# First attention's softmax two tiles ahead with exponentials per head, and one bf16 product for an expert bias

## The reference

```python
x = x + tanh(g_xattn[0]) * xattn0(layernorm(x), ctx, ctx, mask, Wq, Wk, Wv, Wo, bo)
# xattn0: 16 heads of 64, 64 keys
dots = einsum('bhid,bhjd->bhij', qh, kh) * d ** -0.5
dots = where(mask, -finfo.max, dots)
attn = softmax(dots); out = einsum('bhij,bhjd->bhid', attn, vh) -> @ Wo + bo
```

```python
expert_out = dispatched @ w_expert + b_expert        # 256 x 256, bias of 256
combined = combine @ expert_out                       # gate * (location < 100)
```

## Time and profile before

| | us |
|---|---|
| median of 3 runs | 954.27 |
| lowest, highest | 948.47, 955.95 |
| profiled execution | 944.84 |
| its span | 943.1 |
| PE, DVE, ACT, POOL busy | 787.4, 630.2, 334.4, 283.0 |

### The profile page before, as it was taken

The page is one execution under the profiler, slowest core; times in us unless marked ns, Lnnn a source line. Parts: engine busy times, 40 slices in busy tenths (PEclk is TensorE's granted clock), DMA queues, the critical chain, the costliest instruction groups (busy, mean ns, idle before and its releaser), DMA issues.

```text
span 943.1 us, 13461 instructions
## 1 busy us (share of the span) xinstructions
PE 787.4 (83%) x4214; PEld 593.6 (63%) x4216; DVE 630.2 (67%) x1698; ACT 334.4 (35%) x622; POOL 283.0 (30%) x284
## 2 busy tenths in 40 slices
PE   7688988965788777589989799978999998779992
PEld 6455656653256656379978676635676675479971
DVE  3678889866997666555637775556757655566646
ACT  2422231225644662134544543312233221235530
POOL 1038113160001556614561111234001234205540
PEclk9998999997999999779999998889999998889995
DMA  8629950000001002247426000051000011224427
GB/s 284 123 92 385 313 187 0 1 1 1 0 1 34 1 0 86 95 122 248 137 80 223 1 1 1 1 179 34 1 1 12 35 45 47 89 58 143 134 85 255
DMA packets 55474, 83.30 MB, mean 88 GB/s; under 512 B 14688, under 2 KB 44384, under 8 KB 55136
## 3 DMA queue, kind: packets, MB, share of 16 engines
q1 hardware_dynamic: 48496, 63.52, 21.8%
q0 software_dynamic: 6912, 18.95, 5.6%
HBM read 61.41 MB, written 37.95 MB: 105 GB/s over the span
## 4 chain that ended last, share of the span: by engine, by line
PE 50%; DVE 24%; ACT 8%; DVEq 6%; issue 6%; DMA 3%; POOL 2%; SPq 0%; ACTq 0%; POOLq 0%
PE sh L701 12%; PE ob L701 12%; PE sh L1077 6%; PE ob L1077 6%; PE pt L669 4%; DVE sm L1801 2%; DVE x L2043 2%; DVE work L1805 2%; DVE work L1793 2%; DVE mx L1791 2%; ACT work L1340 2%; PE pt L701 2%; DVEq L1790 2%; DVE stats L1657 2%; PE pt L1069 2%
## 5 line engine op out<-in xcount | busy, mean ns | idle before, releaser
L701 PE MATMUL sh<-area,xnT 128*128 128x512 f32 (+1 forms) x384 | 138.2, 509 | 7.0 <-issue 4.5
L701 PE MATMUL ob<-area,work 128*128 128x256 f32 x512 | 116.3, 380 | 9.0 <-ACT work L1277 9.0
L534 POOL TENSOR_TENSOR rstd<-var,minush 128x4 f32<-128x4 f32 (+1 forms) x29 | 30.4, 1047 | 303.6 <-DVE var L1664 303.6
L701 PEld LDWEIGHTS ob<-area,work 128*128 128x128 f32 x512 | 96.7, 190 | 34.6 <-issue 22.8
L598 POOL DMA_INDIRECT yt<-xn,work x80 | 76.7, 959 | 122.5 <-ACT xn L1521 106.9
L701 PEld LDWEIGHTS sh<-area,xnT 128*128 128x128 f32 x384 | 64.3, 199 | 59.6 <-issue 56.4
L1340 ACT ACTIVATE work<-work 128x1024 f32<-128x1024 f32 x32 | 33.8, 1058 | 174.5 <-DVE work L1793 93.6
L589 POOL DMA_INDIRECT xg<-area,dest x64 | 63.9, 999 | 70.4 <-DVE dest L2035 53.0
L669 PE MATMUL pt<-ident,work 128*128 128x128 f32 (+1 forms) x292 | 41.9, 284 | 24.7 <-DVE work L1805 10.8
L701 PE MATMUL ob<-area 128*128 128x256 f32 (+1 forms) x152 | 45.2, 458 | 15.8 <-DVE area L2061 9.0
L669 PEld LDWEIGHTS pt<-ident,work 128*128 128x128 f32 (+1 forms) x292 | 33.8, 142 | 32.8 <-issue 14.4
(11 more groups left out here) (298 smaller groups left out, 1664.2 us busy)
## 6 DMA issues: line engine op xcount, KB each, us to landing
work<-xg SPq DMA_DIRECT2D x80, 129.0 KB, 2.3
area<-in_L_ffn_w SPq DMA_DIRECT2D x4, 2048.0 KB, 12.6
area<-yt SPq DMA_DIRECT2D x8, 1024.0 KB, 9.0
area<-in_L_xattn_Wq SPq DMA_DIRECT2D x2, 1024.0 KB, 9.7
x<-in_x SPq DMA_DIRECT2D x1, 2048.0 KB, 15.3
area<-in_L_xattn_Wo SPq DMA_DIRECT2D x2, 1024.0 KB, 16.0
area<-in_L_xattn_Wkv SPq DMA_DIRECT2D x2, 1024.0 KB, 6.3
out<-x SPq DMA_DIRECT2D x4, 512.0 KB, 2.9
```

Of the source, the lines that this page charges most:

```text
L534: pool.tensor_tensor(rstd[:, n], var[:, n], minush[:, n], ALU.pow).then_inc(given, 1)
L701: mm = pe.matmul(o, a, b, start=(k == 0), stop=(k == len(lhs) - 1))
```

## The change

It has two parts.

**First attention.** `attend16` and the exponential are split: stage 0 has functions of its own, stage 6 keeps the old work under the name `attend6`.

- `sh` fills 12 and 13 are now the scores of tiles 0 and 1, 14 to 21 the eight value fills, and from 22 (`FOLDED0`) on the numbers count as before. PE transposes block 0's tokens before the value folding and does the two tiles of scores there.
- DVE masks and takes maxima in two halves of 8 heads each, the first once PE's first half is there (`scored_half`). The maximum is written negated. The subtraction and the sum are gone.
- ACT does 16 exponentials of 128 x 64 a tile, each with the negated maximum as bias and the sum over keys as its accumulator output. The ones of tiles 0 and 1 run between its value evictions.
- In the loop DVE works on scores of tile i + 2 and normalises tile i + 1; both used to be tile i + 1. ACT's exponentials are of tile i + 2.
- `row_max` and `weight_scales` move from the value folding into tiles 0 to 3 of the loop; statistics of blocks 2 and 3 move forward by a few evictions; the next block's normalisation is done at the end of a block for the one after it.
- SP's wait is for `FOLDED0`, 22.

**Stage 5's bias.** In stage 3, after the tables and ahead of the first pair of expert tiles, DVE splits the bias into three bf16 parts, on partitions 0, 32 and 64 of a zeroed 96-row operand (`be2_parts`, in the memory of `bo0`). PE multiplies 96 rows of bf16 ones with it in one product in place of the float32 one of one row.

```diff
+        SCORES0, VALUES0, FOLDED0 = start_of("sh", 0) + 12, start_of("sh", 0) + 14, start_of("sh", 0) + 22
...
-            sp.wait_ge(sh_taken, start_of("sh", 0) + PRE["sh"][0])
+            sp.wait_ge(sh_taken, FOLDED0)
...
+            def scores16(stage, u, j):
+                n, slot = score_fill(stage, u, j)
+                sh_slot(n)
+                for c in range(2):
...
+                    if stage == 0 and c == 0:
+                        mm.then_inc(scored_half, 1)
+                mm.then_inc(sh_full, 1)
...
+                first_norm_T(6, 1)
+                pe.wait_ge(pt_moved, 8)
+                pe.wait_ge(sh_taken, SCORES0)
+                scores16(0, 0, 0)
+                scores16(0, 0, 1)
+                n = VALUES0
                 pe.wait_ge(in_o, loads)
...
             pe.wait_ge(pt_moved, start_of("pt", 5) + PRE["pt"][5])
+            pe.wait_ge(bias_split, 1)
...
-                                     [T(5, b)[:, k, j * P:(j + 1) * P] for k in range(KD)] + [ones[0:1, :]],
-                                     [wexp[:, k * D:(k + 1) * D] for k in range(KD)] + [be2[0:1, :]])
+                                     [T(5, b)[:, k, j * P:(j + 1) * P] for k in range(KD)] + [onesb[0:96, :]],
+                                     [wexp[:, k * D:(k + 1) * D] for k in range(KD)] + [be2_parts[0:96, :]])
...
+            def exps0(i, first, last):
+
+                act.wait_ge(shifted[0], 2 * i + (2 if last > H // 2 else 1))
+                for h in range(first, last):
+                    p = prob[i % 2][:, h * C:(h + 1) * C]
+                    a = act.activation(p, p, ACT.Exp, bias=mx[:, i % 2, h:h + 1], accum_out=sm[:, i % 2, h:h + 1])
+                if last == H:
+                    a.then_inc(exped[0], 1)
...
+                first_norm_move(6, 0)
+                exps0(0, 0, H // 2)
+                exps0(0, H // 2, H)
                 for m in range(MI):
-                    n = n0 + 12 + m
+                    n = VALUES0 + m
...
+                    if m < 4:
+                        exps0(1, 4 * m, 4 * m + 4)
+
+            def attend0():
+                for b in straight:
+                    for j in range(TB):
+                        i = b.u * TB + j
+                        for half in range(2):
+                            n = prob_fill(0, i, half)
+                            move(n, n % 2, probT[:, half * 512:(half + 1) * 512])
+                        if i + 2 < NT:
+                            exps0(i + 2, 0, H // 2)
+                        if j == 1 and b.u + 1 < NB:
+                            norm_move(0, b, 4)
+                        if i + 2 < NT:
+                            exps0(i + 2, H // 2, H)
...
+            def shift0(i):
+
+                n, slot = score_fill(0, i // TB, i % TB)
+                for c in range(2):
+                    q = slice(c * 512, (c + 1) * 512)
+                    p = prob[i % 2][:, q]
+                    dve.wait_ge(*((scored_half, i + 1) if c == 0 else (sh_full, n + 1)))
+                    ins = dve.scalar_tensor_tensor(heads(p), mask[:, i, :].unsqueeze(1).broadcast_to([P, H // 2, C]), -FMAX,
+                                                   heads(sh[slot][:, q]), ALU.mult, ALU.add)
+                    if c == 1:
+                        ins.then_inc(sh_taken, 1)
+                    dve.drain()
+                    dve.tensor_reduce(mx[:, i % 2, c * H // 2:(c + 1) * H // 2], heads(p), AX.X, ALU.max,
+                                      negate=True).then_inc(shifted[0], 1)
+
+            def normalise0(i):
+                p = prob[i % 2]
+                dve.wait_ge(exped[0], i + 1)
+                dve.reciprocal(rsm[:, i % 2, :], sm[:, i % 2, :])
+                dve.drain()
+                dve.tensor_tensor(heads(p), heads(p), over_keys(rsm[:, i % 2, :]), ALU.mult).then_inc(prob_ready[0], 1)
+
+            def attend0():
+                for b in straight:
+                    for j in range(TB):
+                        i = b.u * TB + j
+                        pb = Block(b.u - 1)
+                        if i >= 1:
+                            add(Block((i - 1) // TB), 0, (i - 1) % TB, [(i - 1) % TB])
+                        if i + 2 < NT:
+                            shift0(i + 2)
+                        if i + 1 < NT:
+                            normalise0(i + 1)
+                        if i < 3:
+                            row_max(i)
+                        if i == 3:
+                            weight_scales()
+                        if b.u >= 1 and j == 0:
+                            norm_stats(pb)
+                        if b.u >= 1 and j == 1:
+                            extremes(pb)
+                        if i == 0:
+                            norm_next(0, straight[0], xn_free(0, straight[0], 5))
+                        if j == 3 and b.u + 2 < NB:
+                            norm_next(0, straight[b.u + 1], xn_free(0, straight[b.u + 1], 5))
+                add(straight[-1], 0, TB - 1, [TB - 1])
+                norm_stats(straight[-1])
+                extremes(straight[-1])
...
+            def bias_parts():
+
+                dve.memset(be2_parts[:, :], 0.0)
+                for r, before in ((0, 0), (32, 1), (64, 2)):
+                    row, part = be2[r:r + 1, :], be2_parts[r:r + 1, :]
+                    for _ in range(before):
+                        dve.drain()
+                        dve.tensor_copy(part, row)
+                        dve.drain()
+                        dve.tensor_tensor(row, row, part, ALU.subtract)
+                    dve.drain()
+                    ins = dve.tensor_copy(part, row)
+                ins.then_inc(bias_split, 1)
...
             fold16(0, bo0, {5: lambda: first_stats(straight[0]), 8: lambda: first_stats(straight[1]), 9: first_norm,
-                            10: row_masks, 13: lambda: first_stats(straight[2]), 14: lambda: row_max(0),
-                            15: lambda: row_max(1), 16: lambda: row_max(2), 17: weight_scales,
-                            18: lambda: first_stats(straight[3])})
-            attend16(0)
+                            10: row_masks, 12: lambda: normalise0(0), 13: lambda: first_stats(straight[2]),
+                            15: lambda: first_stats(straight[3])})
+            attend0()
```

## The result

| | before | changed |
|---|---|---|
| median of the runs (us) | 953.74 (948.47 to 955.95, 4 runs) | 923.95 (915.80 to 925.28, 4 runs) |
| the profiled execution, its span (us) | 944.84, 943.1 | 925.28, 923.5 |

The ratio of the times is 0.968, 95% interval 0.961 to 0.975: the change takes 29.8 us away, and the time is 3 us under the forecast. A second series of the changed kernel has 921.79 us against 954.80, ratio 0.964 (0.959 to 0.970). The 954.80 is the median of eleven executions, three of which were slow (one took 4316.54 us); the other eight, which the ratio uses, have a median of 953.96. The two spans differ by only 19.6 us: the profiled execution of before was 9 us under the median of its kernel, and that of after was the longest of its four. So the traces are compared stretch by stretch.

The account below looks back on a forecast made before the run. VectorE was taken to bound the first attention's loop, TensorE stage 5. Savings 5.0 + 14.4 + 7.8 = 27.2 us took the span from 943.1 to 915.9; with 11.2 for the median, 927 us, range 916 to 942.

Parts of the forecast that it names:

- Part 1: First attention's loop: TensorE sets the pace at 7.76 us a tile, loop 125.0 us against 139.4, 14.4 us saved.
- The margin: Loop handoff: VectorE has the next tile's probabilities ready at 7.5 us, TensorE wants them at 7.76, a quarter microsecond spare.
- Rival (a): Loop: VectorE's handoff is late, 0.5 us a tile over, 7 us in all, giving 934 us; chance 0.16.
- rival (b): Loop: ScalarE becomes the bound, activation and accumulator read not overlapping, 0.52 us a pair, giving 949 us; chance 0.09.
- Part 2: Start, before the loop: first transposes at 69.3 us instead of 74.28, 5.0 us saved (2.3 to 7.3).
- the walk: Start: three engine queues followed through scores and value fills; fills end at 68.0, last eviction 69.2, first transposes 69.3.
- Rival (d): Start saving lost to value folding behind ScalarE's exponentials, or GpSimd 2 us late, giving 932 us; chance 0.07.
- Part 3: GpSimd's weight rounding: scales come about 102 instead of 59, last rounding 1.3 us late but covered, cost 0 (0 to 2).
- Part 4: Stage 5's bias product: one bf16 pass over 96 rows saves 0.48 us in each of 16 products, 7.8 us.
- the 0.17 us kept back for a change between kinds of product: Stage 5: deducted from the 0.65 us a product saving, for a cost of changing product kinds that stays.
- Rival (c): Stage 5: the bias product saves nothing, since switching between kinds of product may be what costs, giving 935 us; chance 0.08.
- The bias's split: Stage 3 on VectorE: some 4.5 us within an 8.72 us wait for gathered tokens; cost 0, or 4.5 without that wait.

Follow-up runs that it names:

- the experiment: One more half-width maximum, result unused, ahead of each reciprocal, against the changed kernel: loop 128.6 us instead of 124.8; whole kernel 924.53 us, a single execution, beside 957.31.
- the bias part alone: The kernel before with only stage 5's bias product changed (with its split into parts): 929.65 us beside 946.97, ratio 0.982.
- the repetition: The changed kernel, unaltered, run once more beside a further variant on the same chip: 921.79 us, ratio 0.964 to the kernel before.

## Why the prediction was right, and where its sum was not

**Part 1, the loop (14.4 us forecast, 14.6 measured).** The mechanism held: 7.76 us a tile, no wait at the handoff, 0.76 us a half instruction, and a tail of 11.8 us (185.92 to 197.74). Two small terms missed and cancelled: the 0.7 us for the moved row maxima came to nothing, and a block end cost 1.40 us and not 1.25 (the transposes and a wait of 0.33 us). The upper bound of a half instruction had 0.15 us for a strided write, which no run shows. The margin was put at 0.26 us; the trace leaves 0.32, and the experiment says that 0.21 of it could be used. Rival (a) needed a handoff longer than that, and only the experiments with work put back ahead of it had one.

**ACT's pairs (rival (b)).** ACT's timeline, from the middle of sixteen in a row:

```profile
51.28 0.33 ACT L1321 ACTIVATE work<-work,mx 128x64 f32<-128x64 f32 x1
51.52 0.19 ACT L1321 ACTIVATION_READ_ACCUMULATOR work<-work,mx 128x1 f32 x1
51.61 0.33 ACT L1321 ACTIVATE work<-work,mx 128x64 f32<-128x64 f32 x1
```

The starts stay 0.33 us apart, as in the earlier trace rows, so sixteen are 5.3 us. In the kernel before one exponential did the tile:

```profile
95.01 1.06 ACT L1340 ACTIVATE work<-work 128x1024 f32<-128x1024 f32 x1 [0.49 <-DVE work L1793]
```

The Trainium skill (VectorE: DVE Perf Modes, The TRN2 errata) advises tiles of 512 elements or more, since each small one pays the latency again. The trace agrees that the small ones cost more: sixteen of 64 elements take 5.3 us where one of 1024 took 1.06. The kernel is faster all the same, since ACT had that room and DVE and the ring did not. The measured pitch is 0.02 us under the estimate of 0.353 us from the Trainium skill (ScalarE: Activation LUTs, Rules for kernel authors).

**Part 2, the start (5.0 us forecast, 1.4 measured in this pair of traces).** This term was mis-sized. The first transposes came at 72.93 and not at 69.3, and the step that failed is that PE was walked through the start at full clock. Granted clock of PE, the last key fill and block 0's transposes, then from the third value fill on, in the changed kernel (length, busy us with the number of matmuls, clock, DMA share, GB/s):

```profile
40.65:45.11 4.46, 3.79 (x17) 0.62 1.06 304
57.56:61.10 3.54, 3.54 (x9) 0.54 0.00 0
```

And in the kernel with one row of bf16, whose start is the same code:

```profile
40.56:43.80 3.24, 2.23 (x16) 1.00 1.10 296
56.26:60.40 4.14, 3.98 (x16) 1.00 0.00 0
```

Of the 3.6 us, 1.8 lie before the value fills, which began at 52.08 and not at 50.3: the last key fill came 0.65 us later than in before (40.65 against 40.00), and from it to the first scores it was 4.46 us, where it is 3.24 at the upper level. The other 1.85 lie in the folding, 20.85 us against 19.0. Six traces share this folding: in four PE ran at the lower level behind the wait of 1.87 us, and it took 20.85 us; in two PE kept the upper level, and it took 19.56. So 1.3 us go with the clock. Of the 0.55 left, 0.4 is the wait for the last eviction, 1.68 us where the walk had 1.3. With the clock up the walk was good: that other kernel has its first transposes at 70.34.

The start also varies more than its saving. The same six traces have their first transposes between 70.34 and 75.09 us, 72.5 in the mean; in three of the ten executions with the new order the first 16 passes of scores took 9.65 us and not 7.13, again at the lower level. The old start came at 74.28 in before and at 77.16 in the bias part alone. The means are 3.2 us apart. Rival (d) had the loss but not its cause: ACT, at 61.11, waited 3.29 us for PE, and not PE for ACT's exponentials.

**Part 3, GpSimd.** POOL's timeline, to be read beside the earlier trace rows:

```profile
106.23 1.25 POOL L564 TENSOR_SCALAR area<-area,qw 128x256 f32<-128x256 f32 x1 [38.33 <-DVE qd L2317]
...
195.30 1.98 POOL L568 TENSOR_SCALAR area<-area 128x704 bf16<-128x704 f32 x1 [0.15 <-issue]
```

Scales reached POOL 4 us later than forecast, the last rounding ended at 197.28, and PE's weight transposes start at 197.74, right behind the loop; PE's wait of 7.54 us behind them is as long as before. Cost 0, and even the 1.3 us of lateness did not come.

**Part 4, stage 5 (7.8 us forecast, 16.1 measured).** The step that failed is the price of a product, and one term was missing. The product saves 0.60 us, not 0.48: the 0.17 us kept back for a change between kinds of product was too much. By blocks the shorter products bring 10.1 us, 16 x 0.60 and a little at the block's seams. The other 6.0 us are the clock: the two blocks with products at the lower level lasted 3.1 and 2.9 us more. The granted clock of 0.88 stood in the earlier trace rows and was given no price; the forecast had the whole stretch as PE's own work at one pace. That the product over one row goes with the fall could not be read from these rows, that the stretch was not at full clock could. Rival (c), nothing saved, took the 0.37 us over six passes for a cost of switching that stays; with one bf16 pass over 96 rows the product takes 1.06 us, 0.05 above the forecast's 1.01 for the bare passes.

**The bias's split.** It took 4.2 us on DVE (390.07 to 394.26), inside the wait of the earlier trace rows. That wait is 8.8 and 9.2 us in the two other traces without a split, 3.6 to 5.4 in six with one, and gone in three, that of the changed kernel among them. There ACT's copy, for which DVE would have waited, had been ready since 392.92, so the split cost 1.3 us. The cover was real, and smaller than the row of one execution let think.

**The sum.** 1.4 + 14.6 + 16.1 = 32.1 us of the two spans' stretches, against 27.2 forecast, and 29.8 between the medians (32.2 in the repetition, from 953.96 us). Of the 12.5 us that the rest of after's trace is longer, 4.6 lie between the loop's end and stage 3's first pair, 1.5 from there to stage 5, 6.4 behind it. The first of these stretches, from the loop's end to DVE's first xnTR of stage 3, lasts about 192 us in the three traces without a split and 192.7 in that with one row of bf16, which has it. It lasts 195.6 us and more in the others. The lag arises in stages 1 and 2, ahead of the split in DVE's queue (in the trace of after behind a series of DVE's idle times of about 1 us with no releaser), so it isn't the split's own time; what it is stays open, and so do the 6.4 us behind stage 5, where the change touches nothing. That the forecast came within 3 us is in part luck: two misses of opposite sign, -3.6 and +8.3, lie in it, and the clock is in both. It cost at the start, where the changed kernel ran at the lower level, and it gave in stage 5, where the old one had.

## What to carry over

Between two engines that each work through a queue in order, look for the ring before you add up busy time: the handoff of one tile plus all that the queue puts ahead of it must fit in the other engine's tile, and a look-ahead only helps if it does. Work that leaves the ring pays even when the engine that takes it then needs five times as long (5.3 us a tile for 1.06 here), as long as that engine has room. And where a stretch's granted clock is below 1.00 with an engine near full, price the clock as a term of its own; where your own order puts new waits ahead of an engine, allow for it there too.

## What the runs showed of the hardware

A product over one row of the contraction, placed between full ones, went with a fall to TensorE's lower clock level in stage 5 of three traces of three, each time with no wait just ahead; over 64 or 96 rows in none of nine. One row of bf16 cost 0.19 us more than 96 rows (1.25 against 1.06 us a product), and float32 took 1.66 us with one row and 1.67 with 64, so fewer rows did not make a product shorter. The same folding took 20.85 us in four traces in which PE ran at the lower level after a wait of 1.87 us, and 19.56 in two in which it kept the upper one after the same wait. And an activation of 64 columns and the read of its accumulator overlap through sixteen in a row: 0.33 us a pair, where the durations add to 0.52.
